# Filling an expert layer's slots by indirect reads from an index table, in place of zero fill and indirect writes of rows

## Chip, cores and metric

The program runs on one core of one Trainium2 chip. The metric is device time in microseconds (us) of one execution; lower is better. Engines are called PE (TensorE), DVE (VectorE), ACT (ScalarE), POOL (GpSimd) and SP (SyncE); a q behind a name is the engine's own instruction queue, where DMAs are issued.

## What is computed

The input is `x` and a context, both 8 x 256 tokens of 256 numbers. Two layers follow each other; the change is in the first, in its mixture of experts (cut from the reference, with T = 2048 tokens, 32 experts, 4 chosen per token):

```python
scores = jax.nn.softmax(xf @ Wg, axis=-1)
weights, indices = jax.lax.top_k(scores, TOP_K)
...
C = CAP_FACTOR * P // E
for e in range(E):
    pos = jnp.nonzero(pair_expert == e, size=C, fill_value=P)[0]
    ...
    xg = xf[tok]
    out = swiglu(xg, W1[e], W2[e], W3[e]) * w[:, None]
    y = y.at[tok].add(out)
z = swiglu(xf, Ws1, Ws2, Ws3)
return (y + z).reshape(B, S, D)
```

Beside it the first layer has an attention with gates before the experts; the second has a long convolution of the context (by a Fourier transform), two small feed-forward blocks, and eight large experts applied densely, which take most of the time. The convolution does not depend on the first layer, and the kernel runs it beside the routing.

## The kernel before, in words

Each engine has one program, written out by hand, and waits for the others on semaphores; an engine does its instructions strictly in the written order, and so does each queue of DMAs.

**Start.** POOL clears part of `eS`, and SP writes it 16 times to DRAM to clear `slots_in` (L413 to L416), 96 tiles of 128 slots, each slot one row of 256 numbers. Attention runs until about 157 us. ACT scales the rows of the first layer into `xn` (L1250); PE turns them and makes the router's logits.

**Routing.** DVE picks four experts a token and counts; a loop over the four choices k (L732 to L737) works out each token's slot, `idS`. When round k is out (`slots_done`), POOL sends 16 indirect writes (L1648), each of 128 rows of `xn` to their slots, and after each fourth waits until they have landed. POOL does 32 of them, the normalisation's affine step for the third quarter of the context (`affine(2)`, L1660 and L1661, which waits for ACT's scaling L1325), 8 more, `affine(3)`, and the last 24.

**Shared expert and table.** Meanwhile PE does `up(0)` and `up(1)` of the shared expert (L1921), 12 idle products (`spare(4, 12)`, L1719), turns two table columns to a row (L1949), and goes on with the eight shared steps; DVE's part of a step is L663, L668, L810. DVE also writes the table `words` that tells PE which expert each pair of tiles uses (L763 to L780).

**Convolution.** Six products on DVE (L836 to L843) alternate with transforms on PE (L1969, L1985); ACT copies the results (L1336, L1330). It ends with `inv_copied`.

**Tile stage.** 96 tiles are worked off as 48 pairs, expert by expert. ACT loads a pair of `slots_in` (L1361), once all scatters have landed; PE turns it (L2008), multiplies by the expert's first weights (L2028), later by the last (L2047, two pairs behind); ACT stores `slots_out`. The weights come through a staging buffer `eS` of three (SP, L434, which waits for the split of the expert two places before) and are split into high and low parts by POOL, two instructions an expert (L1633, L1635), into a ring of six; from the seventh expert on POOL first waits until PE has finished the expert six places before (L1631). Expert 3's split, the fourth, also waits for the end of the convolution's products.

**After it**, POOL gathers the rows back (L1687), DVE adds them, and the second layer follows. None of that is changed.

The lines the change and the prediction touch are in `block.sync` (L413 to L434), `block.vector` (L550, L629, L732 to L737, around L806), `block.scalar` (L1359 to L1399), `block.gpsimd` (L1564, L1640 to L1674) and `block.tensor` (L1946, L1955). The scatter reads:

```python
for _ in range(count):
    k, n = sent[0] // NT, sent[0] % NT
    if n == 0:
        pool.wait_ge(slots_done, k + 1)
    pool.indirect_dma_start(xs_d, ..., xn[:, n, :], ...).then_inc(scattered, 16)
    sent[0] += 1
    if sent[0] % 4 == 0:
        pool.wait_ge(scattered, 16 * sent[0])
```

## Time and profile before

| | |
|---|---|
| time of three runs, median | 1803.61 us (1801.79 to 1805.92) |
| profiled execution: first to last instruction | 1787.3 us |
| PE busy | 93% of the span |
| DVE, ACT, POOL busy | 68%, 27%, 27% |
| mean granted TensorE clock | 0.971 |
| chain that ended last | PE 80%, DVE 6%, issue 4%, POOL 4%, DMA 4% |

The profile has one execution, for which it gives the span but no run time of its own; the median lies 16.3 us above the span. Numbers such as 348.38 in a timeline are us from the span's start. A group of instructions shows how many there are, their busy time and mean length in ns, and the idle time of the engine before them with what ended it.

### The profile page before, as it was taken

The numbers are of one execution on the slowest core, as the hardware profiler recorded it, in microseconds if no ns is written. First come the engines' busy times: TensorE is split into PE (matmuls) and PEld (weight loads), VectorE is DVE, ScalarE is ACT, GpSimd is POOL, SyncE is SP. The second block draws the span as 40 slices with busy tenths as digits, with TensorE's granted clock in tenths as the row PEclk, the third lists the DMA queues.
The fourth block names the chain that finished last, engine by engine and source line by source line (L and its number), as shares of the span: only waits on it lengthen the run. The fifth ranks groups of instructions, "written<-read, shape, count | busy, mean of one in ns | idle before, by whom it ended". The sixth has DMA issues, their size and how long they took to land.

```text
span 1787.3 us, 29133 instructions
## 1 busy us (share of the span) xinstructions
PE 1667.1 (93%) x9784; PEld 1439.4 (81%) x9785; DVE 1207.9 (68%) x2483; ACT 474.6 (27%) x836; POOL 471.5 (26%) x355
## 2 busy tenths in 40 slices
PE   6998987799956898999999999999999999999998
PEld 5997673388854787888888888888888888888887
DVE  6457777556656895666666766766766766766765
ACT  3445322134432464211211211211111111111111
POOL 4274257688426601100100100100100100100100
PEclk9998999899978998999999999999999999999999
DMA  9200022278643200000000000000000000000001
GB/s 368 91 1 30 16 73 96 89 250 272 200 127 119 72 1 19 19 36 18 19 34 18 20 33 18 21 32 18 21 32 18 23 30 18 26 27 18 18 0 48
DMA packets 53827, 106.53 MB, mean 60 GB/s; under 512 B 6528, under 2 KB 37696, under 8 KB 53632
## 3 DMA queue, kind: packets, MB, share of 16 engines
q1 hardware_dynamic: 19920, 63.33, 10.4%
q10 hardware_dynamic: 27696, 25.51, 4.5%
q0 software_dynamic: 6144, 16.79, 2.9%
q8 instruction: 43, 0.70, 0.2%
q14 instruction: 24, 0.20, 0.0%
HBM read 69.96 MB, written 35.65 MB: 59 GB/s over the span
## 4 chain that ended last, share of the span: by engine, by line
PE 80%; DVE 6%; issue 4%; POOL 4%; DMA 4%; ACT 2%; SPq 0%; POOLq 0%; DVEq 0%; another core or an unknown queue 0%; ACTq 0%
PE ps L1921 39%; PE ps L1937 20%; PE ps L2028 4%; DMA slots_in<-xn,idS 2%; POOL slots_in L1648 2%; PE ps L2047 2%; PE ps L1772 2%; PE ps L2103 1%; PE ps L2125 1%; PE ps L2008 1%; DVE x L917 1%; DMA x<-in_x 1%; PE ps L1773 1%; PE ps L1789 1%; PE ps L1790 1%
## 5 line engine op out<-in xcount | busy, mean ns | idle before, releaser
L1921 PE MATMUL ps<-xTH,wH 128*128 128x512 f32 x1024 | 402.5, 393 | 2.1 <-DVE hF L1161 2.1
L1921 PE MATMUL ps<-xTH,wL 128*128 128x512 f32 x1024 | 402.2, 393 | 0.0
L1921 PE MATMUL ps<-xTL,wH 128*128 128x512 f32 x1024 | 398.9, 390 | 0.0
L1309 ACT ACTIVATE sg<-ps 128x512 f32<-128x512 f32 x264 | 157.9, 599 | 885.3 <-PE ps L1921 885.3
L1161 DVE TENSOR_TENSOR hF<-sg,ps 128x512 f32<-128x512 f32 x256 | 175.7, 686 | 302.1 <-ACT sg L1309 302.1
L1620 POOL TENSOR_TENSOR wL<-wS,wH 128x1536 fp32r<-128x1536 f32 x32 | 111.9, 3496 | 959.8 <-ACT wH L1304 959.8
L1937 PE MATMUL ps<-wL,hH 128*128 128x256 f32 x1024 | 289.8, 283 | 0.0
L1937 PE MATMUL ps<-wH,hL 128*128 128x256 f32 x1024 | 289.7, 283 | 0.0
L1937 PE MATMUL ps<-wH,hH 128*128 128x256 f32 x1024 | 288.6, 282 | 0.5 <-DVE hL L1170 0.5
L1170 DVE TENSOR_TENSOR hL<-hF,hH 128x512 fp32r<-128x512 f32 x256 | 258.0, 1008 | 0.1
L1921 PEld LDWEIGHTS ps<-xTL,wH 128*128 128x128 f32 x1024 | 192.8, 188 | 42.2
L1180 DVE SCALAR_TENSOR_TENSOR x<-ps,cw,x 128x256 f32<-128x256 f32 x512 | 222.6, 476 | 1.0 <-PE ps L1937 1.0
L1921 PEld LDWEIGHTS ps<-xTH,wH 128*128 128x128 f32 x1024 | 193.6, 189 | 36.1 <-ACT sg L1309 1.9
L1921 PEld LDWEIGHTS ps<-xTH,wL 128*128 128x128 f32 x1024 | 193.8, 189 | 30.5
L1937 PEld LDWEIGHTS ps<-wH,hH 128*128 128x128 f32 x1024 | 195.5, 191 | 10.6 <-DVE hL L1170 0.7
L1937 PEld LDWEIGHTS ps<-wH,hL 128*128 128x128 f32 x1024 | 195.5, 191 | 9.8
L1937 PEld LDWEIGHTS ps<-wL,hH 128*128 128x128 f32 x1024 | 195.5, 191 | 0.0
L1164 DVE CAST hH<-hF 128x512 fp32r<-128x512 f32 x256 | 109.3, 427 | 38.8 <-PE ps L1937 30.2
L1648 POOL DMA_INDIRECT slots_in<-xn,idS x64 | 76.6, 1197 | 59.6 <-DMA slots_in<-xn,idS 29.7
L2028 PE MATMUL ps<-eHL,hH 128*128 x384 | 81.5, 295 | 2.2 <-POOL eHL L1635 2.2
L1687 POOL DMA_INDIRECT yg<-slots_out,idG x48 | 50.0, 1041 | 69.2 <-DMA slots_out<-yo 49.0
L603 DVE SCALAR_TENSOR_TENSOR Cm<-ps,Dm 128x384 f32<-128x384 f32 x64 | 35.6, 557 | 47.1 <-ACT Dm L1272 43.0
(385 smaller groups left out, 2525.4 us busy)
## 6 DMA issues: line engine op xcount, KB each, us to landing
wS<-in_w SPq DMA_DIRECT2D x32, 768.0 KB, 4.3
slots_in<-eS SPq DMA_DIRECT2D x16, 768.0 KB, 20.2
eS<-in_wr SPq DMA_DIRECT2D x32, 384.0 KB, 3.9
xl<-slots_in ACTq DMA_DIRECT2D x48, 256.0 KB, 3.9
slots_out<-yo ACTq DMA_DIRECT2D x48, 256.0 KB, 3.1
cx<-in_ctx SPq DMA_DIRECT2D x1, 2048.0 KB, 10.4
x<-in_x SPq DMA_DIRECT2D x2, 1024.0 KB, 13.8
out<-x SPq DMA_DIRECT2D x4, 512.0 KB, 2.9
```

The lines of the kernel that those rows point to most:

```text
L1161: dve.tensor_tensor(hF[:, b, :], sg[:, b, :], ps[:, 2 + b, :], ALU.mult).then_inc(mul_done, 1)
L1164: dve.tensor_copy(hH[:, b, :], hF[:, b, :]).then_inc(h_high, 1)
L1170: dve.tensor_tensor(hL[:, b, :], hF[:, b, :], f32(hH[:, b, :]), ALU.subtract).then_inc(h_low, 1)
L1180: dve.scalar_tensor_tensor(x[:, tile, :], acc, cw2[:, tile, bass.ds(it, 1)], x[:, tile, :], ALU.mult, ALU.add).then_inc(evac_done, 1)
L1309: act.activation(sg[:, b, :], ps[:, b, :], ACT.Silu).then_inc(silu_done, 1)
L1620: pool.tensor_tensor(blocks(wL, slot, plain), blocks(wS, slot, plain), f32(blocks(wH, slot, plain)), ALU.subtract).then_inc(w_low, 1)
L1648: pool.indirect_dma_start(xs_d, bass.IndirectOffsetOnAxis(ap=idS[:, n, k:k + 1], axis=0), xn[:, n, :], None, bounds_check=TILES * P - 1, o ...
L1687: pool.indirect_dma_start(slot_rows(n)[:, k, :], None, ys_d, bass.IndirectOffsetOnAxis(ap=idG[:, n, k:k + 1], axis=0), bounds_check=TILES ...
L1772: pe.matmul(ps[:, i % 2, 0:256], kT[:, c, t0:t0 + P], qM[:, i % 12, :], start=True, stop=True)
L1921: last = pe.matmul(ps[:, 2 * half + b, :], piece(w, s, slot, col, P), v[:, k, g * 512:(g + 1) * 512], start=q == 0, stop=q == 5)
L1937: last = pe.matmul(o, h[:, b, t * P:(t + 1) * P], piece(w, s, slot, col, D), start=(opens and t % 2 == 0 and q == 0), stop=(closes and q = ...
L2028: last = pe.matmul(ps[:, 2 + b, t * D:(t + 1) * D], h[:, b, (2 * t + k) * P:(2 * t + k + 1) * P], eFlat[:, bass.ds(off + (w + k * D), D)], ...
```

## The change

The zero fill of `slots_in` and the 64 indirect writes go. In their place:

- SP writes `xn` to a DRAM table `rows`, four DMAs of 512 KB.
- In each round k of DVE's slot loop, the slot number is cut into a tile (`tilef`, slot over 128) and a row (`rowf`, slot modulo 128), and DVE makes 16 one-hot matrices of 128 x 128 in one instruction (`inRow`: is this the row?).
- POOL makes 16 matrices of 128 x 96 a round, one instruction each (`inTile`: the token's number where the tile matches, else 0).
- PE multiplies them, 16 products a round summed over all 64 in one PSUM bank; the sum is the token's number of each slot (row 0 for an empty one). DVE copies it to `idT` before the first shared step. `inRow` and `inTile` have two buffers each. The 12 idle products go.
- POOL fills pairs of tiles with two indirect reads a pair from `rows` into `landing`, a ring of four pairs in SBUF; SP writes each landed pair to `slots_in`. 4 pairs come before `affine(2)`, 16 more after `affine(3)`, 12 before expert 3's split, and 2 before the split of each of experts 6 to 13.
- SP does the first 20 pairs' stores before it loads the first experts' weights, and the later ones between those loads. ACT's load of a pair waits for that pair's store alone.

The diff, cut to its core:

```diff
@@ -24,6 +24,7 @@
 EPS = 1e-5
+EARLY, MIDDLE = 20, 32
 ARENA = 212800 // 64 * 64
@@ -160,6 +161,14 @@
         hC = at("hC", [P, B, 512], F32, start["xn"])
+        inRow = at("inRow", [P, 2, NT, P], F32R, start["xn"])
+        landing = at("landing", [P, 4, 2, D], F32, start["xn"])
+        inTile = at("inTile", [P, 2, NT, TILES], F32R, start["vext"])
+        idT = at("idT", [P, TILES], U32, start["wg0"])
+        rowf = at("rowf", [P, NT, TOPK], F32, start["wg0L"])
+        tilef = at("tilef", [P, NT, TOPK], F32, start["gwt"])
+        token = at("token", [P, NT], F32, end["tilef"])
+        shifted = at("shifted", [P, 2, NT], I32, end["token"])
@@ -381,6 +396,10 @@
+        def filled_before(e):
+            return EARLY if e < 3 else min(MIDDLE + 2 * max(e - RING + 1, 0), PAIRS)
         def f32(ap):
@@ -410,10 +429,6 @@
-            sp.wait_ge(zero_done, 1)
-            zv = xs_d.rearrange("(a p c) d -> a p (c d)", p=P, c=UW // D)
-            for a in range(TILES * D // UW):
-                sp.dma_start(zv[a], eS[:, 0:2, :].rearrange("p i c -> p (i c)")).then_inc(zeros_stored, 16)
@@ -423,13 +438,27 @@
-            sp.wait_ge(zeros_stored, 16 * (TILES * D // UW))
+            rv = xr_d.rearrange("(n p) d -> p n d", p=P)
+            for g in range(4):
+                sp.wait_ge(rows_normed, 4 * g + 4)
+                sp.dma_start(rv[:, 4 * g:4 * g + 4, :], xn[:, 4 * g:4 * g + 4, :]).then_inc(rows_stored, 16)
+            xsv = xs_d.rearrange("(q t p) d -> q p t d", t=2, p=P)
+            def store_pairs(first, last):
+                for q in range(first, last):
+                    sp.wait_ge(pair_landed[q % 4], q // 4 * 32 + 32)
+                    sp.dma_start(xsv[q], landing[:, q % 4, :, :]).then_inc(pair_filled[q % 4], 16)
+            store_pairs(0, EARLY)
             sp.wait_ge(filter_moved, 1)
...
             for e in range(E0):
+                if e >= 4:
+                    store_pairs(filled_before(e - 4), filled_before(e - 3))
                 wait(sp, ew_ready, e - 2)
@@ -734,7 +764,16 @@
                 link(dve.tensor_reduce(slk[:, :, k], sc1[:, :, :], AXX, ALU.add))
-                dve.tensor_copy(idS[:, :, k], slk[:, :, k]).then_inc(slots_done, 1)
+                link(dve.tensor_copy(idS[:, :, k], slk[:, :, k]))
+                dve.tensor_scalar(shifted[:, 0, :], idS[:, :, k].bitcast(I32), 7, None, ALU.logical_shift_right)
+                link(dve.tensor_scalar(shifted[:, 1, :], idS[:, :, k].bitcast(I32), P - 1, None, ALU.bitwise_and))
+                dve.tensor_copy(tilef[:, :, k], shifted[:, 0, :]).then_inc(slots_done, 1)
+                link(dve.tensor_copy(rowf[:, :, k], shifted[:, 1, :]))
+                if k == 0:
+                    dve.wait_ge(rows_stored, 64)
+                wait(dve, part_indexed, k - 1)
+                dve.tensor_tensor(inRow[:, k % 2, :, :], tilen[:, :].unsqueeze(1).to_broadcast([P, NT, P]),
+                                  rowf[:, :, k:k + 1].to_broadcast([P, NT, P]), ALU.is_equal).then_inc(rows_marked, 1)
             link(dve.tensor_scalar(okk[:, :, :], slk[:, :, :], 0.5 * FAR, None, ALU.is_lt))
@@ -804,6 +843,8 @@
             table_columns()
+            dve.wait_ge(part_indexed, TOPK)
+            dve.tensor_copy(idT[:, :], ps[:, 6, 0:TILES]).then_inc(index_read, 1)
             for i in range(8):
@@ -1356,8 +1397,9 @@
-            def load_pair(q, ring):
+            def load_pair(q, ring, filled):
                 wait(act, tT_done, q - 3)
+                act.wait_ge(pair_filled[ring], filled)
                 act.dma_start(xl[:, ring, :, :], pair_of(xsv, q)).then_inc(tile_loaded[ring], 16)
@@ -1379,15 +1421,14 @@
-            act.wait_ge(scattered, 64 * 16)
             act.wait_ge(evac_done, 4 * M_FA)
...
             for q in range(4):
-                load_pair(q, q)
+                load_pair(q, q, 16)
             for q in range(2):
                 tile_high(q, q)
-                load_pair(q + 4, q)
+                load_pair(q + 4, q, 32)
             tile_silu(0, 0)
@@ -1637,21 +1677,24 @@
             pool.tensor_tensor(sL[:, :], sS[:, :], f32(sH[:, :]), ALU.subtract).then_inc(w_low, 1)
-            pool.wait_ge(zeros_stored, 16 * (TILES * D // UW))
-            def scatter(count):
-                for _ in range(count):
-                    k, n = sent[0] // NT, sent[0] % NT
-                    if n == 0:
-                        pool.wait_ge(slots_done, k + 1)
-                    pool.indirect_dma_start(xs_d, bass.IndirectOffsetOnAxis(ap=idS[:, n, k:k + 1], axis=0), xn[:, n, :], None,
-                                            bounds_check=TILES * P - 1, oob_is_err=False).then_inc(scattered, 16)
-                    sent[0] += 1
-                    if sent[0] % 4 == 0:
-                        pool.wait_ge(scattered, 16 * sent[0])
-            sent = [0]
+            for k in range(TOPK):
+                pool.wait_ge(slots_done, k + 1)
+                wait(pool, part_indexed, k - 1)
+                for n in range(NT):
+                    last = pool.tensor_scalar(inTile[:, k % 2, n, :], tilen[:, 0:TILES], tilef[:, n, k:k + 1], token[:, n:n + 1],
+                                              ALU.is_equal, ALU.mult)
+                last.then_inc(tiles_marked, 1)
+            pool.wait_ge(index_read, 1)
+            pool.wait_ge(rows_stored, 64)
+            def fill(first, last):
+                for q in range(first, last):
+                    wait(pool, pair_filled[q % 4], 16 * (q // 4))
+                    for t in range(2):
+                        pool.indirect_dma_start(landing[:, q % 4, t, :], None, xr_d,
+                                                bass.IndirectOffsetOnAxis(ap=idT[:, 2 * q + t:2 * q + t + 1], axis=0),
+                                                bounds_check=NT * P - 1, oob_is_err=False).then_inc(pair_landed[q % 4], 16)
@@ -1661,14 +1704,15 @@
-            scatter(32)
+            fill(0, 4)
             affine(2)
-            scatter(8)
             affine(3)
-            scatter(NT * TOPK - 40)
+            fill(4, EARLY)
             pool.wait_ge(table_done, 1)
...
             for e in range(E0):
+                if e >= 3:
+                    fill(filled_before(e - 1), filled_before(e))
                 if e == 3:
@@ -1943,7 +1987,13 @@
             up(1, 1, 0, None, 0)
-            spare(4, 12)
+            for k in range(TOPK):
+                pe.wait_ge(tiles_marked, k + 1)
+                pe.wait_ge(rows_marked, k + 1)
+                for n in range(NT):
+                    last = pe.matmul(ps[:, 6, 0:TILES], inRow[:, k % 2, n, :], inTile[:, k % 2, n, :], start=k == 0 and n == 0,
+                                     stop=k == TOPK - 1 and n == NT - 1)
+                last.then_inc(part_indexed, 1)
             pe.wait_ge(cols_done, 1)
@@ -1955,6 +2005,8 @@
                     j = i - 1
+                    if j == 2:
+                        pe.wait_ge(index_read, 1)
                     down(j, j, j // 2, None, j // 2 % 2, j % 2 == 0, j % 2 == 1)
```

## Rows read from the trace of the kernel before

**Rows 1.** Busy time in one stretch: us, each engine's busy time (instructions), granted clock, DMA share, GB/s.

```profile
410.00:481.00 71.00, 65.45 (x534) 63.03 (x533) 46.92 (x89) 28.78 (x66) 54.17 (x33) 1.00 0.80 247
```

**Rows 2.** Chain of waits in order of time: start, duration, what.

```profile
348.38 2.42 DMA slots_in<-xn,idS
...
358.04 2.92 PE ps L2028 x12
```

**Rows 3.** Timeline of ACT, last inverse copies: start, duration, [idle before <- releaser].

```profile
349.03 2.06 ACT L1330 ACTIVATE dcw<-ps 128x512 f32<-128x512 f32 x4 [24.12 <-PE ps L1985]
```

**Rows 4.** Timeline of POOL, tile stage: splits that waited for experts 13 and 23 to end.

```profile
422.01 1.47 POOL L1633 TENSOR_TENSOR eHL<-eS,zcol 128x768 fp32r<-128x768 f32 x1 [0.19 <-PE ps L2047]
...
460.41 1.47 POOL L1633 TENSOR_TENSOR eHL<-eS,zcol 128x768 fp32r<-128x768 f32 x1 [0.46 <-PE ps L2047]
```

**Rows 5.** Timeline of PE: first product of the seventeenth pair.

```profile
408.98 0.36 PE L2028 MATMUL ps<-eHL,hH 128*128 x1
```

**Rows 6.** Timeline of DVE: end of the slot loop, first and second shared products.

```profile
218.98 0.19 DVE L738 TENSOR_SCALAR okk<-slk 128x64 f32<-128x64 f32 x1
...
226.28 0.69 DVE L663 TENSOR_TENSOR hF<-sg,ps 128x512 f32<-128x512 f32 x1 [3.17 <-ACT sg L1309]
...
227.46 0.69 DVE L810 TENSOR_TENSOR hL<-hF,hH 128x512 fp32r<-128x512 f32 x1
...
231.03 2.69 DVE L788 BATCH_NORM_STATS2 st<-zn 128x6 f32<-128x256 f32 x8
233.75 0.69 DVE L663 TENSOR_TENSOR hF<-sg,ps 128x512 f32<-128x512 f32 x1
```

**Rows 7.** Timeline of PE: the 12 idle products behind up(1).

```profile
228.17 2.12 PE L1719 MATMUL ps<-maskT,idb 128*128 128x384 bf16 x12
```

**Rows 8.** Instruction groups: small copies on POOL (busy us, mean ns, idle before).

```profile
L1583 POOL COPY qM<-qT 32x256 f32<-32x256 f32 x64 | 25.7, 401 | 37.2 <-ACT qT L1215 17.9 <-PE ps L1773 15.9
...
L1574 POOL COPY gateW<-gwt 128x32 f32<-128x32 f32 x16 | 2.5, 204 | 0.1
```

**Rows 9.** Timeline of DVE in the convolution, with and without POOL beside it.

```profile
274.04 4.35 DVE L836 TENSOR_TENSOR tv<-Zs,WG 128x2048 f32<-128x2048 f32 x1 [4.39 <-ACT Zs L1336]
...
293.70 3.25 DVE L842 TENSOR_TENSOR tv<-tv 128x1024 f32<-128x1024 f32 x1
296.98 2.71 DVE L843 TENSOR_TENSOR PI<-tv 128x512 f32<-128x512 f32 x1
...
308.40 1.22 DVE L842 TENSOR_TENSOR tv<-tv 128x1024 f32<-128x1024 f32 x1
309.65 0.69 DVE L843 TENSOR_TENSOR PI<-tv 128x512 f32<-128x512 f32 x1
```

**Rows 10.** Timeline of ACT: third and fourth scaling of the context rows.

```profile
253.53 2.07 ACT L1325 ACTIVATE zn<-zn,sd,rs 128x256 f32<-128x256 f32 x4
...
257.70 2.07 ACT L1325 ACTIVATE zn<-zn,sd,rs 128x256 f32<-128x256 f32 x4
```

**Rows 11.** Timeline of POOL: an affine step's second half and the scatter behind it.

```profile
295.94 3.20 POOL L1661 TENSOR_TENSOR zn<-zn,bcv 128x1024 f32<-128x1024 f32 x1
299.94 3.04 POOL L1648 DMA_INDIRECT slots_in<-xn,idS  x1 [0.80 <-POOL zn L1661]
```

**Rows 12.** Instruction group on POOL, 299 to 350 us alone: the last 24 scatters.

```profile
L1648 POOL DMA_INDIRECT slots_in<-xn,idS x24 | 32.8, 1366 | 17.4 <-DMA slots_in<-xn,idS 11.2 <-issue 5.5 <-POOL zn L1661 0.8
```

**Rows 13.** Instruction groups on POOL, whole span: gathers and an expert's split.

```profile
L1635 POOL TENSOR_TENSOR eHL<-eS,eHL 128x768 fp32r<-128x768 f32 x32 | 58.7, 1833 | 2.5
L1687 POOL DMA_INDIRECT yg<-slots_out,idG x48 | 50.0, 1041 | 69.2 <-DMA slots_out<-yo 49.0 <-issue 14.6 <-DVE x L917 3.0
L1633 POOL TENSOR_TENSOR eHL<-eS,zcol 128x768 fp32r<-128x768 f32 x32 | 47.0, 1469 | 13.9 <-PE ps L2047 12.3 <-DMA slots_in<-xn,idS 1.5
```

**Rows 14.** DMA issues: engine, count, KB each, us to landing.

```profile
eS<-in_wr SPq DMA_DIRECT2D x32, 384.0 KB, 3.9
...
slots_out<-yo ACTq DMA_DIRECT2D x48, 256.0 KB, 3.1
...
yg<-slots_out,idG POOLq DMA_INDIRECT x48, 2.8
```

22 lines of the change are left out of this document (14 added, 8 removed).

## Prediction

> **What bounds the kernel now.** I read the busy time by stretch first. Between 410 and 481 us, in the tile stage, PE works 65 of 71 us and DVE 47, but POOL too works 54 [rows 1]: it splits the experts' weights and has 17 us left. The reader should see here that POOL, with 27% of the span, is nearly full where the change gives it work. Next the chain of waits: up to 350.8 us it runs through the scatters, the last issued at 348.38 with its landing, and so names them as the bound [rows 2]. But the timeline of ACT shows the other string beside it: the last inverse copies of the convolution run from 349.03 to 351.1, after 24 us in which ACT waited for PE and DVE [rows 3], and PE's first transposes wait for them too. The two strings end within 0.4 us. So taking the scatters away alone is worth almost nothing there. Then the timelines of the tile stage: experts 13 and 23 are released to POOL at 422.01 and 460.41 [rows 4], 3.84 us an expert; a split is 1.47 + 1.83 us and the gap between, 3.35 in all [rows 13]. POOL is faster than PE by half a microsecond an expert, no more. Expert 13's first tile is in the seventeenth pair, whose first product starts at 408.98 [rows 5]; that is my yardstick below.
>
> **The index table.** Each round of DVE's loop gets an instruction over 2048 elements with two SBUF inputs, 2.4 us by L842's 1.22 for 1024 [rows 9], and four small ones of 0.2 us (L738 is one of these [rows 6]): 3.2 a round, 12.8 in all. The loop ended at 218.98 [rows 6], so DVE is done with it at 231.8 at the earliest. POOL gets 64 instructions of 96 elements: copies of 32 and of 256 elements take 0.20 and 0.40 us [rows 8], I take 0.26, or 4.2 us a round. PE comes to the first part when up(1) is through, at 228.2, where the idle products stood [rows 7]; 12 of those took 2.12 us for 384 columns, so 16 products of 96 columns lie between 1 and 2.8 us a part; I take 2. With two buffers each, rounds 0 and 1 are marked by then, but POOL can begin round 2 only when PE's first part is through, at 230.2. Beside DVE I give its rounds 5.5 us: 236 and 242, PE's last part 244, the index read at 245. Unhindered it would be 240; at 0.6 us for each mark, 254.
>
> The second shared product stood at 233.75. It now follows the index by one shared step (226.28 to 228.15, 1.9), the statistics (231.03 to 233.75, 2.7) and two small copies of 0.25, 5.1 us in all [rows 6]: 250.1, so this whole string is **16.4 us later**. The 3.2 us that DVE idled ahead of its first shared product are in this figure. The row table's four stores lie in front of that with the queue empty, and PE's wait at `j == 2` is long met: nothing.
>
> **What the convolution gives back.** Where POOL's affine steps lie beside the products, DVE's instructions take 2.05 us more: 2.71 for 0.69, 3.25 for 1.22, and 4.35 for the one of double that size [rows 9]. POOL now does these steps before the products: 6.1 us back. The chain then ends at 351.1 + 16.4 - 6.1 = 361.4. Experts 0 to 2 are split by then, so PE's first product follows after 5.5 us and not 6.9: 366.9 for 358.04 [rows 2]. The chain alone costs **+8.9 us**.
>
> **POOL's new list.** Eight indirect reads from 245.3; the nearest rows are the gathers, 1.04 in the mean, some of them beside DVE's adds [rows 13], with 0.30 of issue ahead of each (the last 24 scatters show 5.5 us of it [rows 12], for the 18 that did not wait): I take 1.30 each, done at 255.7. Then POOL stands still for `affine(2)`, behind which 16 pairs are queued: ACT's third scaling ended at 255.6 and the fourth at 259.8 [rows 10], now 272.0 and 276.2; two affine steps of 4.7 (each half 2.35, longer beside DVE [rows 11]) end at 282. The next 32 reads lie beside the convolution. There the last 24 scatters took 1.37 + 0.30 = 1.67 each [rows 12], and one of 3.04 began just as DVE's 2.3 us product did [rows 11]; bounds 1.30 and 1.67, I take 1.6: 333.2. SP holds the first experts' weights behind the twentieth pair's store: landing 2.8, a store's issue and two loads' 1.5, weights 3.9 [rows 14] make 8.2: 341.4. Three splits: 351.5. The ring of four is no bound if landing 2.8, issue 0.5 and store 3.1 [rows 14], 6.4, stay under three pairs of 2.6.
>
> Now comes what nothing hides. Twelve pairs stand before expert 3's split: 24 x 1.30 = 31.2, 382.7; three splits, 392.7. PE ran out of experts at about 367 + 3 x 3.84 = 378.5. Then two pairs and a split for each of experts 6 to 13: 4 x 1.30 + 3.35 = 8.55, against PE's 3.84; eight times 68.4: **461.1**. From expert 14 POOL needs 3.35 again and PE 3.84, so PE makes nothing up and loses nothing more. The yardstick moves from 409.0 to 461.1: +52.1 us.
>
> A rule from the Trainium skill weighs on one choice. What the rows show: beside DVE's products from SBUF, POOL's DMA issue and DVE hold each other up by 2 us [rows 9, 11], yet in the tile stage, where every DVE input pair has one in PSUM, all 32 splits kept their length (1.47, 1.83) with DVE busy two thirds [rows 1, 13]; hence 1.30 and not 1.67 there. The Trainium skill, "SBUF — State Buffer", section "SBUF: two separate sides", says that the port pair shared by the two is an exclusive lock for a whole instruction, taken by a DVE operation with two SBUF inputs against a GpSimd operation that reads SBUF. By it the reads in the tile stage stay at 1.30, as the sum has them, but each of POOL's marks can also wait behind the 2.4 us row marks, which would move the index from 245 towards 254, and the sum with it by up to 9 us.
>
> **Sum.** 1787.3 + 52.1 = 1839.4 for the profiled span; the median lies 16.3 above the span before, so 1855.7. The zero fill gives nothing: it overlaps attention, whose engines do not wait for it. Bounds: with the index at 240 (-5), 1.30 beside the convolution (-10) and a quicker weight load (-2) it is +35; with 254 (+9), 1.67 everywhere (+2 and 56 x 0.37 = +21), +84. The likeliest case's own range is 1838 to 1888.
>
> **Rivals.** *The cover holds* (0.09): the reads in the tile stage fit into POOL's spare time and only the chain's +8.9 is left, 1812. For it: POOL idles some 17 of 71 us there. Against: 32 reads in eight experts are 42 us where the spare time is eight times 0.5. *The ring binds* (0.05): a pair's store is held behind weight loads in SP's queue, and each of the 28 late pairs costs the whole trip of 6.4 and not 2.6: +106 more, 1962. Against: only four pairs are in flight and SP is ordered so that they go first. *Faster* (0.07): the marks hide in waits DVE and PE had (3.2 and 2.1 us), the index is there by 233, and POOL keeps up. Then the second shared product is at 238.1, +4.4; minus 6.1 from the convolution and 1.4 at the first product gives -3.1; if POOL's freedom from waits for its scatters also helps, -5: 1799 to 1800. It decides at an index before about 236, and DVE alone needs till 231.8 and PE starts at 228.2; it also needs the cover. The same place with the index at 236 gives no change (0.04). That the work removed is not truly removed can be excluded by the diff: both DMAs are gone.
>
> **How the numbers follow.** The likeliest case has 0.75. No change means within 0.2%, 3.6 us, about what a measurement of this kernel can tell. Faster 0.06, same 0.05, slower 0.89. The range reaches from below the likeliest case's low end towards the held cover, 1824, to 1886; it leaves out the ring case, the faster ones and most of the held cover. I give 1855.
>
> **What would show it.** The profile after should have: the copy to `idT` at about 245; POOL idle 255 to 272 before its affine step; DVE's products without the lengthened ones; the last inverse copy at about 361; POOL without a gap from 341 on, reading, then splitting; PE waiting in the tile stage for POOL's split of experts 3 and 6 to 13, some 45 us in all, with expert 13's split ready at 461; the tile stage's end near 566 where it was near 514. I am wrong if PE's waits for POOL there are under 10 us, if an indirect read costs well under 1.3 us of POOL, or if the index comes before 236.

## The result, and the profile after

The changed kernel takes **1892.59 us** (median of 4 runs, 1888.62 to 1894.15), the kernel before, on the same chip, 1804.76 (1801.79 to 1813.10, 4 runs): ratio 1.0477, 95% interval 1.0450 to 1.0503. It is slower, as forecast, but by 88 us and not by some 50, outside the range given.

The instructions of the index table after (POOL's marks in one line, then POOL and DVE at the second round's row marks, then PE):

```profile
L1684 POOL TENSOR_SCALAR inTile<-tilen,tilef,token x64: 681/696/3327, 210.6 to 262.8; 128x96 fp32r<-128x96 f32 x64
...
215.44 4.76 POOL L1684 TENSOR_SCALAR inTile<-tilen,tilef,token 128x96 fp32r<-128x96 f32 x3
...
215.99 2.29 DVE L775 TENSOR_TENSOR inRow<-tilen,rowf 128x2048 fp32r<-128x2048 f32 x1
...
226.94 1.99 PE L1994 MATMUL ps<-inTile,inRow 128*128 128x96 f32 x16 [0.97 <-POOL inTile L1684]
240.09 3.65 PE L1994 MATMUL ps<-inTile,inRow 128*128 128x96 f32 x16 [11.16 <-POOL inTile L1684]
...
263.59 3.65 PE L1994 MATMUL ps<-inTile,inRow 128*128 128x96 f32 x16 [7.06 <-POOL inTile L1684]
```

A mark takes 0.70 us in the median (shortest, median, longest in ns stand behind the count), all 64 of them 53 us; PE waits for them before every part. Four marks took 2.8 to 3.3 us, each one that ran beside DVE's row marks (three marks from 215.44 on take 4.76 us together); taken from start to start, the marks are 0.67 us apart, 43 us for 64, and some 10 us come on top at those four places. The index is copied at 267.28, where I had 245, and the second shared product starts at 272.23 (233.75 in [rows 6]). Then POOL's timeline, cut at the places of the prediction's list:

```profile
294.42 2.39 POOL L1703 TENSOR_TENSOR zn<-zn,bcv 128x1024 f32<-128x1024 f32 x1 [15.53 <-ACT zn L1366]
...
364.34 1.98 POOL L1673 TENSOR_TENSOR eHL<-eS,zcol 128x768 fp32r<-128x768 f32 x1 [9.35 <-DMA eS<-in_wr]
366.40 2.66 POOL L1675 TENSOR_TENSOR eHL<-eS,eHL 128x768 fp32r<-128x768 f32 x1
...
378.97 1.29 POOL L1695 DMA_INDIRECT landing<-rows,idT  x1
...
414.07 1.48 POOL L1673 TENSOR_TENSOR eHL<-eS,zcol 128x768 fp32r<-128x768 f32 x1
...
424.29 1.01 POOL L1695 DMA_INDIRECT landing<-rows,idT  x1
...
492.36 1.81 POOL L1675 TENSOR_TENSOR eHL<-eS,eHL 128x768 fp32r<-128x768 f32 x1
```

Eight reads end at 278.9, POOL stands idle for ACT's third scaling, 32 reads end at 355.0, the first split waits for its weights, 24 reads end at 414.05, and from 424.29 each of experts 6 to 13 costs four reads and a split, 8.47 us. Expert 13's split ends at 494.16, **494.2**; the yardstick before was 409.0. What this does to PE, in the busy time by stretch (after the stretch's bounds: length, then busy time of PE, weight loads, DVE, ACT and POOL, granted clock, DMA share, GB/s), and in PE's waits (total, times, longest):

```profile
414.00:495.00 81.00, 53.77 (x329) 48.93 (x330) 30.87 (x59) 19.52 (x45) 69.16 (x56) 0.83 0.92 234
495.00:565.00 70.00, 64.31 (x512) 61.89 (x511) 43.99 (x84) 27.57 (x63) 58.03 (x36) 0.98 0.85 268
```

```profile
PE ps L1994 <- POOL inTile L1684: 28.3, 4, 11.2
PE ps L2080 <- POOL eHL L1675: 20.5, 7, 5.0
PE ps L2037 <- DVE PI L884: 15.7, 4, 11.6
```

While the reads last, PE is busy 54 of 81 us at a granted clock of 0.83; behind them the stretch looks like [rows 1] again. The first product of the seventeenth pair, the yardstick of the prediction, starts at 494.39. The last split ends at 557.4 and the tile stage near 601, 87 us later than before. The profile's chain of work has 9% of the span on POOL.

The profiled execution before was a quick one, quicker than every timed run of that kernel (the quickest took 1797.27). PE's wait for `xTL` behind the tile stage was 1.6 us in it; a pause in the same place is 10.4 after, and in three other profiles of kernels with the old scatter this wait is 9.4 to 11.1. So the two spans (1787.3 and 1886.8) differ by 99.5, the medians by 88, and the yardstick by 85; I reason with the last two. POOL's share of the span before was 26%, where the prediction and the table ahead of it say 27%; nothing hangs on it.

### The profile page after: what moved, and what is told of

It is laid out like the page before. It is cut to its first block, busy times and chain, and to the rows that moved or that the text cites. A ratio compares the mean times of both kernels' runs of the same rounds, so it can differ in the third digit from the quotient of the medians.

```text
span 1886.8 us, 29470 instructions
## 1 busy us (share of the span) xinstructions
PE 1696.2 (90%) x9836; PEld 1467.0 (78%) x9837; DVE 1227.8 (65%) x2505; ACT 474.4 (25%) x836; POOL 557.4 (30%) x450
## 3 DMA queue, kind: packets, MB, share of 16 engines
q1 hardware_dynamic: 32784, 65.43, 10.4%
## 4 chain that ended last, share of the span: by engine, by line
PE 74%; POOL 9%; DVE 6%; issue 5%; DMA 3%; ACT 2%; SPq 0%; POOLq 0%; DVEq 0%; another core or an unknown queue 0%; ACTq 0%
PE ps L1965 38%; PE ps L1981 19%; POOL landing L1695 3%; POOL inTile L1684 3%; PE ps L2080 2%; PE ps L1816 2%; PE ps L2099 2%; PE ps L2177 2%; PE ps L2155 1%; DMA landing<-rows,idT 1%; POOL eHL L1673 1%; POOL eHL L1675 1%; DMA slots_in<-landing 1%; DMA x<-in_x 1%; PE ps L1817 1%
## 5 line engine op out<-in xcount | busy, mean ns | idle before, releaser
L1695 POOL DMA_INDIRECT landing<-rows,idT x96 | 107.2, 1117 | 37.0 <-issue 26.8
L2080 PE MATMUL ps<-eHL,hH 128*128 x384 | 87.6, 310 | 22.8 <-POOL eHL L1675 20.5
L2080 PEld LDWEIGHTS ps<-eHL,hH 128*128 128x128 f32 x384 | 68.3, 205 | 25.8 <-issue 25.6
```

The lines of the kernel that those rows point to most:

```text
L1695: pool.indirect_dma_start(landing[:, q % 4, t, :], None, xr_d, bass.IndirectOffsetOnAxis(ap=idT[:, 2 * q + t:2 * q + t + 1], axis=0), boun ...
L2080: last = pe.matmul(ps[:, 2 + b, t * D:(t + 1) * D], h[:, b, (2 * t + k) * P:(2 * t + k + 1) * P], eFlat[:, bass.ds(off + (w + k * D), D)], ...
```

## The experiments

Ratios compare each variant with the kernel before on the same chip, whose medians were 1806.33 (7 runs), 1804.67 (7), 1804.17 (23) and 1802.65 (17). The time at which the index arrives moves from kernel to kernel by up to 5.6 us with nothing changed ahead of it (266.8 to 272.4), so I compare stretches inside a trace as well as medians.

### The marks on DVE

```diff
+                link(dve.tensor_tensor(inTile[:, k % 2, :, :], tilen[:, 0:TILES].unsqueeze(1).to_broadcast([P, NT, TILES]),
+                                       tilef[:, :, k:k + 1].to_broadcast([P, NT, TILES]), ALU.is_equal))
+                dve.tensor_tensor(inTile[:, k % 2, :, :], f32(inTile[:, k % 2, :, :]), token[:, :].unsqueeze(2).to_broadcast([P, NT, TILES]),
+                                  ALU.mult).then_inc(tiles_marked, 1)
...
-                for n in range(NT):
-                    last = pool.tensor_scalar(inTile[:, k % 2, n, :], tilen[:, 0:TILES], tilef[:, n, k:k + 1], token[:, n:n + 1],
-                                              ALU.is_equal, ALU.mult)
```

> The changed kernel, but the tile marks are made by DVE, two instructions over 1536 elements a round, and not by 64 instructions on POOL (53 us there in the changed kernel's trace). Theory 1 (POOL's marks hold back the index, and the index everything behind it): the copy to the index comes at about 249 and not 267 us, expert 13's split is ready 18 us earlier (476 for 494), and the time falls by about 18 us, to some 1874. Rival (the index is held by PE or DVE themselves, so moving the marks onto DVE only lengthens its loop): the index comes no earlier and the time stays within 5 us or rises.

Measured: 1871.88 us (1870.66 to 1876.66), ratio 1.0375 [1.0337, 1.0414]. Its trace has two instructions over 1536 elements a round in place of POOL's sixteen:

```profile
240.58 1.75 DVE L777 TENSOR_TENSOR inTile<-tilen,tilef 128x1536 fp32r<-128x1536 f32 x1
242.37 1.76 DVE L779 TENSOR_TENSOR inTile<-inTile,token 128x1536 fp32r<-128x1536 f32 x1
...
247.91 0.24 DVE L851 CAST idT<-ps 128x96 uint32<-128x96 f32 x1
```

The index comes 19.4 us earlier and the kernel takes 20.7 less. So the marks on POOL stood in the one chain of work that sets the time (the string), and what they lost there came off in full.

### No index at all

This kernel leaves the index out: DVE writes made-up row numbers in one instruction, nothing is marked and PE makes no parts; the 12 idle products stand again; rows are read, stored and multiplied as many times as in the changed kernel.

```diff
-            dve.tensor_copy(idT[:, :], ps[:, 6, 0:TILES]).then_inc(index_read, 1)
+            dve.tensor_scalar(idT[:, :], tilen[:, 0:TILES], 16.0, tc[:, 0:1], ALU.mult, ALU.add).then_inc(index_read, 1)
```

> The changed kernel without the index: no marks, no products on PE, the old slot loop and the 12 idle products; the reads go to made-up rows (16 times the tile plus the partition), so the slots' contents are not the routed rows. It prices reads and stores alone. Theory 1 and 2 together: reading starts at about 224 us, expert 13's split is ready at about 452 for 494, so 42 of the 88 us are the index and 46 the reads: time about 1850. Rival (the reads in the tile stage do not bind, only the delayed string of shared steps and convolution does): with that string undelayed the time is within 5 us of the kernel before.

Measured: 1849.39 us (1845.56 to 1853.82), ratio 1.0250 [1.0212, 1.0289]; expert 13's split is ready at 451.8. So 43 us of the 88 are the index, and 45 are the reads: even an index for nothing leaves a loss nearly as large as the 52 us that my sum had for both.

### One operation in a mark

```diff
-                    last = pool.tensor_scalar(inTile[:, k % 2, n, :], tilen[:, 0:TILES], tilef[:, n, k:k + 1], token[:, n:n + 1],
-                                              ALU.is_equal, ALU.mult)
+                    last = pool.tensor_scalar(inTile[:, k % 2, n, :], tilen[:, 0:TILES], tilef[:, n, k:k + 1], None,
+                                              ALU.is_equal)
```

> The changed kernel, with POOL's marks made by the comparison alone, without the product with the token's number (the index then holds 0 or 1 instead of the row's number, so all reads fetch rows 0 and 1; nothing else is left out). It prices the mark, which took 0.70 us where the prediction had 0.26. Theory 1 (the cost is fixed in issuing and in fetching a pointer operand; the second operation and its pointer are a part of it): a mark takes 0.35 to 0.5 us, the index is read some 15 to 20 us earlier, and the kernel takes 15 to 20 us less, near 1875. Theory 2 (the mark is set by its 96 columns in four byte numbers, whatever is done to each): still 0.65 to 0.7 us, and the time within 3 us. Reads that all fetch two rows could also be quicker or slower to land than reads of scattered rows: the time of one read shows that apart.

Measured: 1892.17 us (1889.67 to 1893.69), ratio 1.0468 [1.0413, 1.0524]. A mark is 0.52 us, and the index comes 9.0 us earlier, at 258.26. Yet the time did not move: the gain went in waits. The first split waited 10.8 us for its weights, and from 372 on POOL waited for places in the landing buffer, 10.4 us in six waits (longest 5.0), most of it (8.1) between the splits of experts 2 and 3. The four long marks beside DVE's row marks cost the same 10 us as before. The reads, which here all fetch rows 0 and 1, were also slower to carry out, and the likely reason is that they fetch the same two rows: in the stretch of the 24 reads between experts 2 and 3, the packets of POOL's queue (count, MB, share of the 16 DMA engines' time) took 47.3% here (372 to 413, first line) and 28.2% after (379 to 415, second line).

```profile
q0 software_dynamic: 1016, 2.80, 47.3%
...
q0 software_dynamic: 1114, 3.06, 28.2%
```

So the kernel serves to price a mark, but not as a test of the time.

### Where the reads stand in the list

Three kernels differ from the changed one in two numbers, the pairs read before the first split and before expert 3's: 20 and 20 in the first, 48 and 48 in the second, 20 and 28 in the third.

```diff
-EARLY, MIDDLE = 20, 32
+EARLY, MIDDLE = 20, 20
```

> The changed kernel without the block of 12 pairs ahead of expert 3's split: from the twentieth pair on, two pairs before each split, of experts 6 to 19. Theory 2 (POOL has one list, and its length up to the last read sets when PE has its experts): expert 13's split is ready 31 us earlier, but the six steps after it are now 8.5 us and not 3.35, so the tile stage ends within 5 us of the changed kernel's. Rival (the block, by its place ahead of expert 3, is what starves PE): the time falls by about 31 us, to some 1862.

Measured: 1910.16 us (1907.18 to 1914.17), ratio 1.0578 [1.0537, 1.0619], 17.6 above the changed kernel: neither. POOL's waits between 300 and 540:

```profile
POOL eHL L1673 <- DVE PI L884: 12.6, 1, 12.6
POOL eHL L1673 <- PE ps L2099: 10.1, 1, 10.1
```

Without reads to do, POOL stood idle for the convolution's end ahead of expert 3 and for expert 0's end ahead of expert 6, and the reads it had put off came in longer steps up to expert 19, whose split ended at 535.5 (517.0 after). These 22.7 us of new idleness more than cover the 17.6 lost; from the index to the last split it is 307.2 us, 17.0 more than after.

> The changed kernel with all 48 pairs filled before the first split: no read stands in the tile stage. Theory 2: POOL's list is as long as before, PE's first expert product comes at about 446 us, after which PE is not starved, and expert 13's first product comes within 8 us of the changed kernel's; time 1885 to 1900. Rival (reads mixed with splits cost more than their sum, by ring waits or the shared port): the time falls by over 15 us.

Measured: 1912.44 us (1908.99 to 1917.52), ratio 1.0601 [1.0559, 1.0642]. All reads first: the first split starts at 460.4, the convolution ended long before, and PE stands idle for 61.8 us in one wait. The splits then come at 3.35 us, but PE is not quick enough to win back what it lost.

> The changed kernel, with 16 reads instead of 24 between the splits of experts 2 and 3, so that the eight others come in steps of four before experts 14 and 15. With 40 and none of them in that place the kernel took 17.6 us more, and POOL stood idle for 12.6 us for the convolution's end and 10.1 us for expert 0. Theory 1 (that list was slower by the idle time it forced on POOL, not by where the reads stand: the convolution's last products end near 387 to 395 and 16 reads end near 404): no idle time, the string to the last expert with reads is as long as before, the paced splits run two experts further, and the time is within 3 us of the changed kernel. Theory 2 (each expert at the longer step costs PE its 5 us whatever POOL does, since fewer experts are ready when PE starts): 6 to 10 us slower.

Measured: 1896.22 us (1892.96 to 1903.96), ratio 1.0524 [1.0477, 1.0571]: 3.6 above the changed kernel, with ranges that overlap, so between the two theories and at most a little slower. There is idle time again, 3.2 us for expert 0 and 6.4 for weights, and the last split ends 2.2 us later. In all four lists a read costs nothing where POOL would otherwise be idle, and what counts is the length of POOL's list with its forced idle time; none of the three others was quicker than the kernel's own.

### The first weights

SP loads the weights of experts 0 to 2 ahead of the stores of most early pairs, behind 4 of them in one kernel and behind 12 in the other (the diff is of the first).

```diff
-            store_pairs(0, EARLY)
+            store_pairs(0, 4)
             sp.wait_ge(filter_moved, 1)
             sp.wait_ge(up_done, 8)
+            for e in range(3):
+                sp.dma_start(eS[:, e % 3, :], dram["wr"][e]).then_inc(estage_loaded[e % 3], 16)
+            store_pairs(4, EARLY)
```

> The changed kernel, with SP loading the weights of experts 0 to 2 as soon as the first four pairs of rows are stored, before the rest of the early pairs, so that they no longer queue behind the reads. Theory 1 (the 9.35 us that the first split waited for its weights stand in the one string that ends at expert 13's split): the split starts behind the last early read, near 355, and the kernel takes 9 us less than the changed one, 1883 to 1886. Theory 2 (the string has slack there, since the splits then fall earlier into the convolution, meet more of DVE's products and give the time back in the port, or the stores of pairs become late in their place): within 3 us of the changed kernel.

Measured: 1892.22 us (1889.48 to 1894.44), ratio 1.0463 [1.0407, 1.0519]. POOL's longest wait between 300 and 375:

```profile
POOL landing L1698 <- DMA slots_in<-landing: 8.3, 4, 7.4
```

SP now stood at `up_done` with the stores behind it, so the ninth of POOL's 32 reads waited 7.4 us for a place. Measured from the index on, the first split starts 4.6 us earlier and expert 13's is ready 3.5 us earlier, yet the median is the changed kernel's to 0.4 us: most of the 9.35 us had moved, not gone.

> The changed kernel, with the weights of experts 0 to 2 loaded behind the stores of 12 of the early pairs of rows. Where they stood behind 4, SP waited for the products' end before it went on to the stores, POOL waited 7.4 us for a free place in the landing buffer in turn, and of the 9.35 us only 4.6 were gained at the first split. Theory 1 (SP's queue in order is all that stands between): by the twelfth pair, near 330, the products are done, neither wait remains, the first split starts 7 to 9 us earlier behind the last read, and the kernel takes 6 to 9 us less than the changed one, 1884 to 1887. Theory 2 (what is gained there is lost as the splits meet DVE's products in the convolution): within 3 us of the changed kernel.

Measured: 1885.13 us (1882.29 to 1887.36), ratio 1.0449 [1.0404, 1.0493], 7.5 less than the changed kernel. POOL's timeline at the end of the 32 reads:

```profile
356.35 1.00 POOL L1698 DMA_INDIRECT landing<-rows,idT  x1 [0.30 <-issue]
357.37 1.48 POOL L1676 TENSOR_TENSOR eHL<-eS,zcol 128x768 fp32r<-128x768 f32 x1
```

Behind 12 neither wait is left: the split follows the last read at once.

### A cheaper split, and the repairs together

The first line added stands from expert 6 on only, where the split waits for a register's value.

```diff
+                    link(pool.tensor_tensor(zcol[:, :], zcol[:, :], zcol[:, :], ALU.add))
-                pool.tensor_tensor(high, eS[:, e % 3, :], zcol[:, :].to_broadcast([P, EW]), ALU.add).then_inc(ew_high, 1)
+                pool.tensor_copy(high, eS[:, e % 3, :]).then_inc(ew_high, 1)
```

> The changed kernel, with the high half of each expert's weights rounded by a copy instead of an addition of a column of zeros. In the trace of the changed kernel that addition takes 1.47 us and the subtraction 1.84. Theory 1 (POOL's string sets the time up to expert 13's split, and a copy with one operand takes about half as long): the split is 2.6 us instead of 3.35, 14 of them stand in the string, so 10 us less, near 1882. Theory 2 (the copy takes what the addition does): within 2 us of the changed kernel. Theory 3 (the copy is quicker, but PE's own work at its lower clock is the bound in those steps): the split is quicker and the time moves by under 4 us.

Measured: 1888.24 us (1884.65 to 1889.31), ratio 1.0443 [1.0387, 1.0499]. POOL's timeline around expert 6:

```profile
431.63 0.21 POOL L1672 TENSOR_TENSOR zcol<-zcol 128x1 f32<-128x1 f32 x1
431.90 0.82 POOL L1674 CAST eHL<-eS 128x768 fp32r<-128x768 f32 x1
432.80 1.83 POOL L1676 TENSOR_TENSOR eHL<-eS,eHL 128x768 fp32r<-128x768 f32 x1
```

The copy takes 0.82 for 1.47, but the small instruction that carries the wait on a register costs 0.3 of it: a step is 8.1 us instead of 8.47. From the index to expert 13's split it is 223.5 us for 226.9, 3.4 less, and the kernel 4.4 less, where theory 1 had 10: the copy is quick, but only part of it reached the step.

> The changed kernel with three repairs together: marks made by DVE, the first weights loaded before the rest of the early pairs, and the high half by a copy. If they all stand in one string, their gains add: 20.7 us for the marks (as measured), 9 for the weights, about 10 for the copies if a copy is quicker, so 1892.6 less 40 is 1853, still 48 above the kernel before. If instead another string is next (the rows of the landing buffer, the convolution's end, PE at its lower clock), the sum falls short: 1862 or more.

Measured: 1866.34 us (1861.60 to 1869.72), ratio 1.0331 [1.0275, 1.0387]. The gains add only in part: 26.3 for the 39.7 expected, because the weights still stood behind 4 pairs (POOL waited for places in the landing buffer 15.0 us in five waits, the longest 7.5) and the copy gave what it gave above. It is the best form of the change that I ran, and 62 us above the kernel before.

### The kernel before, asked the same questions

Could the scatters have been kept and made cheaper? The first kernel waits behind each group of four for the group before the last one (on two semaphores in turn); the second also moves the affine steps to behind 28 scatters; the third moves only these.

```diff
-                    if sent[0] % 4 == 0:
-                        pool.wait_ge(scattered, 16 * sent[0])
+                    if sent[0] % 4 == 0 and sent[0] > 4:
+                        g = sent[0] // 4 - 2
+                        pool.wait_ge(scattered[g % 2], 64 * (g // 2 + 1))
```

> The kernel before, with POOL waiting, behind each group of four scatters, for the group before the last one instead of the last. In its trace POOL waited 29.7 us for landings in 13 waits. The convolution's last inverse copies end at 349 and the last scatter at 350.8, so two strings end together. Theory 1 (the waits for landings stand in POOL's string, but the convolution, with DVE and ACT, ends just as late): the last scatter comes some 15 us earlier and the time stays within 3 us of the kernel before. Theory 2 (POOL's string alone set the start of the tiles): 10 us or more quicker.

Measured: 1830.72 us (1829.55 to 1832.80), ratio 1.0147 [1.0128, 1.0167]: 26.6 us **slower**, which no theory had. POOL issued 32 scatters in one run from 210.56 to 251.94. DVE's timeline, and PE's:

```profile
252.71 0.35 DVE L763 COPY etf<-ps 1x192 f32<-1x192 f32 x1 [27.34 <-remote]
...
227.44 0.49 PE L1951 MATMUL ps<-ident,tc 96*1 96x96 f32 x4
...
236.53 0.59 PE L1923 MATMUL ps<-xTH,sL 128*128 128x512 f32 x1 [1.72 <-issue]
```

DVE's copy needs only PE's four transposes, through at 227.9; it ran 0.8 us behind the run's last scatter. PE, too, paused for nothing that the profile shows. The trace also holds the time of each semaphore increment: the one that tells DVE of the transposes (`rows_turned`) is recorded at 252.69, 24.8 us behind them, and the copy starts 0.02 us later. In the kernel before it is at 230.73, 0.01 us behind the transposes. So it is the signal that was late, not DVE that was busy or held.

> As the one before, and POOL's affine steps of the convolution's normalisation put together behind 28 scatters, off the stretch in which DVE makes its products. Theory 1 (with POOL's string short, the port hold-ups of DVE's products by those affine steps are next, 6.1 us as the prediction had them): 4 to 8 us quicker than the kernel before, 1797 to 1801. Theory 2 (the hold-ups move to DVE's shared steps, as they did in the changed kernel, where the second of them came to 2.3 to 2.4 us for tiny operations): within 2 us of the kernel before, or up to 5 slower.

Measured: 1831.14 us (1828.03 to 1838.05), ratio 1.0154 [1.0131, 1.0178]. The same stall, 21.7 us, ended 0.3 us behind the last of its run of 28 scatters.

> The kernel before with only the order of the affine steps changed as above, the waits for landings left as they were. Theory 1 (both strings end together, so a shorter convolution alone gives nothing): within 2 us of the kernel before. Theory 2 (the convolution alone sets the start of the tiles): as quick as the variant with both.

Measured: 1806.46 us (1798.76 to 1811.48, 12 runs), ratio 1.0010 [0.9994, 1.0026], no change clear of noise: theory 1's number. It is a weak test, since in its trace POOL's last scatter also ends 2.4 us earlier, the last inverse copy 3.7 and the tiles' first product starts 2.6 us earlier (355.5), too little for these medians to show.

Then runs of other lengths: a pause behind every eighth and every sixteenth scatter (`% 8` and `% 16` for `% 4`).

> The kernel before, with POOL waiting for its landings behind every eighth scatter instead of every fourth: half of the pauses go, runs of scatters without a pause become 10 us long. With the wait one group behind, POOL issued 32 scatters in one run of 41 us, DVE stood still for 27.3 us from 225.4 until 0.8 us after the run's last scatter, and the kernel was 26 us slower. Theory 1 (another engine is starved only by a run without a pause that lasts some 20 us or more): DVE goes on as in the kernel before, the last scatter comes some 12 us earlier, the convolution ends as late, and the time is within 3 us of the kernel before. Theory 2 (any longer run starves): DVE's copy of the two turned rows waits for the end of the current run, up to 10 us, and the kernel is 5 to 15 us slower. Theory 3 (the stall had to do with the wait one group behind or its second semaphore, not with the pauses): as the kernel before, and so is the variant with groups of sixteen.

Measured: 1810.67 us (1806.96 to 1817.89, 12 runs), ratio 1.0041 [1.0019, 1.0062], 8.0 us slower.

> As the one before, with a pause behind every sixteenth scatter: runs of 20 us. The first falls from 213 to 234, the second from 236 to 256, over DVE's copy near 230. Theory 1 (a run starves once it is some 20 us long): the copy is late by up to 5 us, since the first run ends near 234, and the kernel is 0 to 6 us slower. Theory 2 (any run starves what needs it while it lasts): the same here, and the variant with groups of eight then has a wait too. Theory 3 (not the pauses): within 2 us of the kernel before.

Measured: 1824.95 us (1817.09 to 1830.03), ratio 1.0113 [1.0077, 1.0150], 22 us slower. DVE's timeline (the small steps of the square root started every 0.21 us before):

```profile
239.54 0.35 DVE L763 COPY etf<-ps 1x192 f32<-1x192 f32 x1 [9.08 <-remote]
...
255.39 0.18 DVE L468 SCALAR_TENSOR_TENSOR nt<-nt,ve 128x16 f32<-128x16 f32 x1 [0.55 <-issue]
256.09 0.18 DVE L469 SCALAR_TENSOR_TENSOR rs<-nt,rs 128x16 f32<-128x16 f32 x1 [0.53 <-DVE nt L468]
```

With 16, DVE first stands for 9.1 us and then goes on at a third of its pace through the second run; with 8 there is no such stall of DVE, and PE shows one unexplained pause of 2.4 us. The traces show by which string the time was lost (us):

| kernel | last scatter ends | last inverse copy ends | first product of the tiles | median, against before |
|---|---|---|---|---|
| before | 349.4 | 351.1 | 358.0 | |
| pause every 8 | 335.4 | 362.0 | 368.1 | +8.0 |
| pause every 16 | 335.6 | 371.6 | 376.6 | +22.3 |
| one group behind, first run of 32 | 337.6 | 380.5 | 385.1 | +26.6 |

POOL's own string did become 12 to 14 us shorter each time, and the tiles started with the convolution, which came 11 to 29 us later. Theory 2 holds for the time (each run longer than four that I tried costs something), theory 1's threshold of 20 us does not, and theory 3 is out for the variants of 8 and 16, which keep the old semaphore and its wait. That the pauses are what keeps the other engines' signals moving is shown by this series; by which way POOL's issuing holds them back is not.

> The kernel before with its zero fill of the slots made twice, one behind the other (12.6 MB more written, at about 0.4 MB a microsecond some 35 us more of the DMA engines, from about 55 to 90). The prediction counted the removal of the fill at nothing. Theory 1 (it lies beside work that needs no transfers): within 2 us of the kernel before. Theory 2 (transfers behind it on the same engines, the filter's and the head's, become late): 3 us or more slower, and the removal would have been worth about as much.

Edit: SP waits for the zero fill and issues all 16 of its stores again; the later waits count to 32. Measured: 1804.96 us (1800.48 to 1812.66, 12 runs), ratio 0.9995 [0.9974, 1.0016]. The trace has the DMA engines at 0.78 between 60 and 100 us, where they idle before, and PE as busy as ever, 40.0 us of 40. Between 0 and 60 the DMA share is 0.92 before and 0.41 after, and PE's busy time 44.7 and 44.6. Filling twice cost nothing that 12 runs show, and the one fill, over by 60 us in the kernel before, kept PE no less busy than none: it was free.

## Why the forecast was right in kind and wrong in size

**Right:** that two strings ended together before, so that shorter scatters alone were worth nothing (12 to 14 us off them never brought the tiles forward; since the convolution was late too each time, this is not shown by itself); that the zero fill gives nothing; that POOL, with reads between the splits, becomes the bound up to expert 13, and that the loss stays about the same from expert 14 on (85 us there, 87 at the end of the tile stage). Expert 13's split tells a variant's time: in the kernels with the changed list the median lies 1393 to 1400 us above it.

| kernel | expert 13 ready | median |
|---|---|---|
| before (first product of pair 17) | 409.0 | 1804.8 |
| no index | 451.8 | 1849.4 |
| all repairs | 466.5 | 1866.3 |
| marks on DVE | 478.9 | 1871.9 |
| weights behind 12 pairs | 489.3 | 1885.1 |
| weights behind 4 pairs | 492.8 | 1892.2 |
| one operation in a mark | 493.2 | 1892.2 |
| after | 494.2 | 1892.6 |
| split by copy | 495.5 | 1888.2 |

**The step that failed** is the price of a mark: "copies of 32 and of 256 elements take 0.20 and 0.40 us [rows 8], I take 0.26, or 4.2 us a round". A mark is no copy: it does two operations and takes two numbers from memory for each partition. It took 0.70 us in the median and 0.83 in the mean, 13.2 us a round. With one operation and one such number less it took 0.52. My own bound of 0.6, "254", was drawn too low, so the range could not hold it. In the string it reads: index at 267.3 for 245, +22.3. Two things are in this figure. The price itself is the larger: 64 marks 0.67 us apart are 43 us where 0.26 makes 17. The other is the hold-up by DVE's row marks, which the prediction had as a possible wait and gave 1.3 us in each of two rounds, with up to 9 in all as the bound: it was 2.5 us in each of four, 10 in all, so this alone used the bound up. In PE's parts I had 2 us, right at the higher clock (1.99) and 1.7 too little for the last one, at the lower.

Four smaller terms make up the rest of 494.2 less 461.1 = 33:

- The first weights: the first split started 9.35 us behind the last read, against 8.2, but the 32 reads with the 0.8 us ahead of them took 50.8 us and not 51.2: together +0.7.
- "Three splits: 351.5": beside DVE's products the three took 14.5 us and not 10, +4.4. I had given them their length from the tile stage, though [rows 9, 11] showed what POOL and DVE do to each other in the convolution.
- 24 reads took 35.1 us and not 31.2, +3.9: three of 1.3, 2.4 and 1.6 us at their head beside the same products, and a gap of 2.1 that the profile books as issue, behind a landing buffer that may have been full.
- Eight steps took 70.1 us and not 68.4, +1.7, of which 2.15 is one wait for a place in the ring; a plain step was 8.47 for my 8.55.

22.3 + 0.7 + 4.4 + 3.9 + 1.7 = 33.0. The other 3 us by which the medians moved further (88 against 85) are within what one execution says of a median.

**"What the convolution gives back"** came out with the wrong sign. The first product moved by 45.3 us (274.04 to 319.29) where the second shared product moved by 38.5, and the last inverse copy ends at 397.6, where I had 361.4. The affine steps did leave the products, but met DVE's small work instead:

```profile
294.49 2.35 DVE L817 TENSOR_SCALAR rt<-rt 1x32 f32<-1x32 f32 x1
...
296.97 2.41 DVE L819 TENSOR_TENSOR words<-words,downw 1x52 int32<-1x52 int32 x1
...
302.06 2.71 DVE L851 TENSOR_TENSOR hL<-hF,hH 128x512 fp32r<-128x512 f32 x1
```

Instructions that take 0.17, 0.19 and 0.69 us alone took 2.35, 2.41 and 2.71, beside POOL's affine steps of 2.35 to 2.43. And the three splits then held the last products, six of 1.7 to 2.7 us. The Trainium skill, "SBUF — State Buffer", section "SBUF: two separate sides", has the shared port pair as an exclusive lock for a whole instruction; by that rule, an instruction of 32 elements on one partition can last 2.4 us, and the trace agrees. It seems to have cost nothing here, since DVE's last product ends at 389.9 and the last inverse copy at 397.6, while PE, done with experts 0 to 2 near 413, waited for POOL's split of expert 3, begun at 414.07; no run tries it apart.

**"The median lies 16.3 above the span before"** was a misreading. A run's time is 1.8 us above its own span in most runs; the profiled execution was one of the quick ones, 14.5 us below the median, of which some 8 are the wait told above and the rest is open. It added nothing false to the sum here, for the yardstick's shift is a difference, but it belongs to the executions and not to the span.

**The list.** I had said that the 24 reads ahead of expert 3 were what "nothing hides". They filled time in which POOL would have stood idle for the convolution: with 12 pairs fewer there POOL idled for 12.6 us. The sum was right for the kernel as it is, since it counted all of POOL's work and found no gap, but read as a price of these reads it was wrong.

**The rivals.** The held cover fell: 20.5 us of PE's waits name POOL's splits, where I had set 10 as the sign of being wrong and put them at some 45; PE's work at the lower granted clock (0.83 from 414 to 495) may fill part of what I had as waits. The ring did not bind, apart from one wait of 2.15 us and perhaps the gap of 2.1. The faster case fell with the index.

## What to carry to other kernels

Price an instruction by a row with the same operation, the same kinds of operand and the same number of operations; where the trace has none, let the upper bound be a multiple, since here 64 short instructions at 0.70 us for 0.26, and what held four of them, were worth 22 us. When an engine's list is rearranged, add up its forced idle time before calling a piece of work free or dear, and follow each wait that is moved into the queue that it then stands in: 9.35 us of weights came back as 7.4 of ring until the load stood at the right pair. And waits that seem to cost 30 us on one engine may be what lets the others run.

## What the runs showed of the hardware

- **A long unbroken run of indirect writes from POOL goes with late signals between the other engines.** Pauses behind every 4, 8 and 16 scatters and a run of 32 cost 0, 8, 22 and 27 us. DVE stood for 27.3 us ahead of a copy of 192 numbers, because the increment that releases it was recorded 24.8 us behind PE's transposes; with 16 it is 6.5 us (233.01 to 239.51), and DVE's own small steps are signalled 0.5 us behind their end for 0.01 before. The lock on the shared ports does not explain it as it is stated: DVE ran many instructions beside earlier scatters of the same run at their usual length, up to 225 us, and PE paused as well, of which the Trainium skill, "SBUF — State Buffer", section "SBUF: two separate sides", says that it never waits on anyone. Instruction loading does not either: none lies between 205.2 and 258.6 in that trace. In the trace after, whose reads run 32 and 16 at a time, no stall of that size stands, but one of the kind does: ACT waited 5.8 us at the end of the 24 reads and went on at 415.46; the PE products that it needs ended at 413.17, their increment is recorded at 415.44. It cost nothing, since PE then waited for POOL anyway. Whether rows read hold less than rows written was not tried, and neither was any run without the profiler's recording, which may have a part in it.
- **PE's clock fell in the index stage and made its own wait longer.** Between 230 and 267 its granted clock is 0.50, that is 1.2 GHz, after it had stood idle for the marks from 228.9; its sixteen products of 96 columns took 3.65 us in place of 1.99 at the higher of its two levels, 1.7 us of that in the string.
- **A reduced split.** A copy that rounds 768 numbers took 0.82 us on POOL, the addition of a broadcast column of zeros 1.47, in the same place of the kernel.
